# Values of two key tiles in a row, and x's rounding moved to ScalarE, in a fused Perceiver kernel

## The reference, cut to what matters

```
# quantised layer (_L0_ffn_ref), on layernorm(x)
scale = 127.0 / clip(max(abs(x), axis=-1), 1e-05)
x_q   = clip(round(x * scale), -128, 127) / scale
h     = (x_q @ w1_q.T) * s1 ; h = new_gelu(h)
out   = (quantised(h) @ w2_q.T) * s2

# large attention (_L1_xattn_ref): 16 heads, 64 queries, 1601 keys
q_r, k_r = rotated, projected queries and keys
attn  = softmax(einsum('bhsr,bhlr->bhsl', q_r, k_r))
ctx_c = einsum('bhsl,bld->bhsd', attn, kv_r)      # the "values"
out   = ctx_c through w_kc_kv and Wo
```

## Time and profile before

| what | us |
|---|---|
| median of 3 runs | 2840.44 |
| the profiled execution | 2837.08 |
| its span | 2835.2 |
| small attention and weights before the quantised layer | 0 to 331 |
| quantised layer | 331 to 466 |
| large attention | 466 to 2074 |
| second small attention | 2074 to 2200 |
| mixture of experts | 2200 to 2835 |

### The profile page before, as it was taken

One profiled execution on the slowest core, in us unless ns is written; L12 is line 12 of the kernel. 1 busy time (PEld: TensorE's weight loads), 2 busy tenths in 40 slices (PEclk: granted clock), 3 DMA queues, 4 the chain that ended last, 5 costly groups with the idle time before them and its releaser, 6 DMA issues. The chain is left out here.

```text
span 2835.2 us, 46672 instructions
## 1 busy us (share of the span) xinstructions
PE 2658.0 (94%) x16872; PEld 1648.4 (58%) x16872; DVE 1529.4 (54%) x2425; ACT 1110.6 (39%) x2096; POOL 1243.3 (44%) x668
## 2 busy tenths in 40 slices
PE   6989467999999999999999999999979899999999
PEld 4667345656655665666566566656446465656555
DVE  4757585565565556456555655655569633323322
ACT  4635363354445435444543544454435311111110
POOL 1033014577687778668766866776500000000000
PEclk9989698999999999999999999999999899999999
DMA  2000400110111101111110110110030111111111
GB/s 65 1 30 0 153 1 35 50 60 30 47 41 47 41 29 59 38 39 41 47 41 29 59 45 31 41 47 30 18 158 0 32 51 49 56 53 56 52 60 41
DMA packets 44051, 128.00 MB, mean 45 GB/s; under 512 B 6596, under 2 KB 11332, under 8 KB 42312
## 3 DMA queue, kind: packets, MB, share of 16 engines
q1 hardware_dynamic: 43032, 126.53, 13.8%
q10 hardware_dynamic: 944, 0.45, 0.1%
HBM read 85.20 MB, written 2.24 MB: 31 GB/s over the span
## 5 line engine op out<-in xcount | busy, mean ns | idle before, releaser
L716 POOL TENSOR_TENSOR cx_acc<-cx_acc,f_w 128x1024 f32<-128x1024 f32 x310 | 736.4, 2375 | 218.0 <-ACT f_w L1070 205.6
L1070 ACT ACTIVATE f_w<-cx_st 128x512 f32<-128x512 f32 x768 | 438.7, 596 | 447.2 <-PE cx_st L911 392.0
L1174 DVE TENSOR_REDUCE cx_mhalf<-cx_mx 128x1 f32<-128x804 f32 x512 | 480.9, 989 | 171.3 <-PE cx_mx L887 171.2
L922 PE MATMUL cx_av<-f_w,cx_kv 128*64 128x512 f32 x1536 | 412.1, 615 | 0.0
L910 PE MATMUL cx_st<-cx_q,cx_k 128*128 128x512 f32 (+1 forms) x832 | 367.4, 442 | 4.1 <-ACT cx_prob L1070 3.4
L911 PE MATMUL cx_st<-cx_q,cx_k 128*128 128x512 f32 (+1 forms) x832 | 328.9, 395 | 0.0
L887 PE MATMUL cx_mx<-cx_kp,cx_q 128*128 128x402 f32 x1024 | 297.2, 376 | 19.5 <-DVE cx_mhalf L1174 18.3
L887 PEld LDWEIGHTS cx_mx<-cx_kp,cx_q 128*128 128x128 f32 x1024 | 167.6, 189 | 200.2 <-DVE cx_mhalf L1174 183.4
L1996 DVE TENSOR_TENSOR moe_passed<-moe_silu,moe_up 128x512 f32<-128x512 f32 x112 | 76.9, 687 | 382.0 <-issue 356.1
L1917 ACT ACTIVATE moe_silu<-moe_gate 128x512 f32<-128x512 f32 x112 | 66.9, 597 | 490.8 <-PE moe_gate L1841 490.8
L910 PEld LDWEIGHTS cx_st<-cx_q,cx_k 128*128 128x128 f32 (+1 forms) x832 | 154.9, 186 | 170.4 <-ACT f_w L1070 136.4
(11 more groups left out here) (216 smaller groups left out, 3766.3 us busy)
## 6 DMA issues: line engine op xcount, KB each, us to landing
cx_k<-cx_kp SPq DMA_DIRECT2D x32, 804.0 KB, 3.9
moe_share<-moe_coef_kept SPq DMA_DIRECT2D x56, 256.0 KB, 3.0
cx_ctx<-in_cx_ctxN SPq DMA_DIRECT2D x32, 416.0 KB, 3.3
cx_ctxr<-in_cx_ctxrN SPq DMA_DIRECT2D x32, 416.0 KB, 3.9
cx_k<-cx_kp SPq DMA_DIRECT2D x32, 402.0 KB, 5.2
moe_wgu<-in_moe_wgu SPq DMA_DIRECT2D x7, 1024.0 KB, 11.0
moe_wd<-in_moe_wd SPq DMA_DIRECT2D x4, 896.0 KB, 22.3
moe_share<-moe_coef_kept SPq DMA_DIRECT2D x16, 224.0 KB, 2.9
```

The lines of the kernel that those rows point to most:

```text
L716: engine.tensor_tensor(acc[rows, :, :], sofar, prob[slot(kt)][rows, :, :], ALU.add).then_inc(s_acc, 1)
L922: last = pe.matmul(av[DCX * p:DCX * p + DCX, :], kv[e][0:nk(kt), kt, :], prob[slot(kt)][0:nk(kt), p, :], start=(kt == 0), stop=(kt == NKT ...
L1070: act.activation(prob[slot(kt)][rows, p, :], st[p][rows, :], ACT.Exp).then_inc(s_exp, 1)
L1174: dve.tensor_reduce(mhalf[:, i // 2, i % 2:i % 2 + 1], mx[i % 2][:, :, 0:KQ], AX.XY, ALU.max)\
```

## The change

In the large attention `VALUES_AT` lists, for even and odd batches, the steps in which `values` is issued. Where the step before is not in the list, its key tile is done first in the same place. Odd batches do the tiles (0,1), (2,3), (4,5), (6,7), (8,9), (10,11) in pairs at the end of steps 1, 3, 5, 7, 9 and 11, and tile 12 alone; even batches do (0,1), (2,3), (4,5) in pairs and 6 to 12 alone. `denominators` stays at the end of step 0.

In the quantised layer the multiplication and the first rounding of x go from VectorE (L1596) to a new `round_x` on ScalarE, with two new semaphores. VectorE's `quantise_x` is cut in two: `find_x_scale(t + 2)` now stands before `unscale(t + 1)`, and the rest of `quantise_x(t + 2)` at the end of the pass, behind `change_x` and `gather`.

```
+    VALUES_AT = ((1, 3, 5, 6, 7, 8, 9, 10, 11, 12), (1, 3, 5, 7, 9, 11, 12))
...
-                            values(n, e, kt)
+                            if kt in VALUES_AT[e]:
+                                if kt - 1 not in VALUES_AT[e] and kt > 0:
+                                    values(n, e, kt - 1)
+                                values(n, e, kt)
...
+            def round_x(t):                                    # ScalarE
+                act.wait_ge(s_xs, t + 1)
+                act.activation(xn[t % 2][:, :], xn[t % 2][:, :], ACT.Identity, bias=bias[:, 0:1],
+                               scale=inv[t % 2][:, 0:1]).then_inc(s_xr, 1)
...
+            round_x(0)
+            round_x(1)
             keep_y1T(0)
             keep_y1T(1)
             gelu(0)
...
                 for n in job_range(t, 0):
                     keep(n)
+                if t + 2 < NT:
+                    round_x(t + 2)
                 keep_y2T(t)
...
-            def quantise_x(t):                                 # VectorE
+            def find_x_scale(t):
...
-                step.done(scales(t, 0))
-                step.done(dve.tensor_scalar(xn[g][:, :], xn[g][:, :], inv[g][:, 0:1], ROUND, ALU.mult, ALU.add))
+                scales(t, 0).then_inc(s_xs, 1)
+
+            def quantise_x(t):
+                dve.wait_ge(s_xr, t + 1)
...
+            find_x_scale(0)
+            find_x_scale(1)
             quantise_x(0)
+            quantise_x(1)
             gather(2)
-            quantise_x(1)
             unscale(0)
             for t in range(NT):
                 find_scale(t)
+                if t + 2 < NT:
+                    find_x_scale(t + 2)
                 if t + 1 < NT:
                     unscale(t + 1)
                 quantise_hidden(t)
-                if t + 2 < NT:
-                    quantise_x(t + 2)
                 if t > 0:
                     change_x(t - 1)
                 if t + 3 < NT:
                     gather(t + 3)
+                if t + 2 < NT:
+                    quantise_x(t + 2)
```

More of the change, by code:

```diff
@@ L1420, in quantised_mlp @@
     s_rstd = sem("f0_rstd")
+    s_xs = sem("f0_x_scale_found")
+    s_xr = sem("f0_x_rounded")
     s_y1 = sem("f0_y1_quantised")
@@ L1586, in gather @@
                 dve.tensor_scalar(mv[t % 2][:, 1:2], mv[t % 2][:, 1:2], EPS, None, ALU.add).then_inc(s_var, 1)
-            def quantise_x(t):
+            def find_x_scale(t):
                 g = t % 2
                 dve.wait_ge(s_rstd, t + 1)
+                if t >= 2:
+                    dve.wait_ge(s_y1, t - 1)
                 step.done(dve.tensor_scalar(xn[g][:, :], x_all[:, t, :], mv[g][:, 0:1], rstd[g][:, 0:1],
@@ L1594, in quantise_x @@
                 step.done(dve.tensor_reduce(amax[g][:, 0:1], xn[g][:, :], AX.X, ALU.max, apply_absolute_value=True))
-                step.done(scales(t, 0))
-                step.done(dve.tensor_scalar(xn[g][:, :], xn[g][:, :], inv[g][:, 0:1], ROUND, ALU.mult, ALU.add))
+                scales(t, 0).then_inc(s_xs, 1)
+            def quantise_x(t):
+                dve.wait_ge(s_xr, t + 1)
                 if t >= 2:
                     dve.wait_ge(s_y1T, t - 1)
-                dve.tensor_scalar(y1[g][:, :], xn[g][:, :], ROUND, 127.0, ALU.subtract, ALU.min).then_inc(s_y1, 1)
+                dve.tensor_scalar(y1[t % 2][:, :], xn[t % 2][:, :], ROUND, 127.0, ALU.subtract, ALU.min)\
+                    .then_inc(s_y1, 1)
             def unscale(t):
```

## The result

| what | before | after |
|---|---|---|
| median of 11 runs each on one chip, us | 2840.44 | 2852.65 |
| lowest to highest | 2835.08 to 2846.61 | 2846.25 to 2861.37 |
| ratio, with its 95% interval | | 1.0046 [1.0033, 1.006] |
| the profiled execution, us | 2837.08 | 2853.11 |
| large attention, first score matmul to the last matmul of the last `denominators` | 1550.8 | 1561.6 |

The forecast was +18, this is +12.

What follows compares the result with a forecast made beforehand. TensorE was taken to bound the large attention. Attention +17 and quantised layer +1 gave +18 on the profiled 2837.08, 2855; the runs' median lies 3.4 higher, so 2858 us, range 2840 to 2872.

Steps and rivals of the forecast that it cites:

- The saving per joint, 0.36: Large attention: joining two values groups saves 0.36 us of TensorE's switching between scores and values, if TensorE never waits.
- The gap of 1.57 in place of 1.03: Steps without values: the next score waits for the exp until 1.57 to 1.74 us; TensorE is ready at 1.03.
- (0,1) gains nothing: Odd batches: joining values 0 and 1 leaves the number of switches the same, as `denominators` then stands alone.
- third rival: Odd steps 0, 1, 2, 4: ScalarE's query copies or the two-wait way back also delay; +42, 2882 us; chance 0.07.
- (6,7), (8,9), even (4,5): the reduces: Joints in steps with pieces: VectorE's reduces hold up TensorE; +0.29, about +0.2 and +0.25 us.
- (10,11), -0.2: Odd batches, no pieces: turned keys of 0.4 us in the gap nearly cover the wait, so -0.2 us.
- The last batch, +1.5: Large attention's last batch: no pieces and no turned keys, so five joints at 0.29 each, +1.5 us.
- The sum of the attention, +17: Large attention: fifteen batch pairs at +1.07 give +16, last batch +1.5, batch 0 -0.4; +17 us, bounds -18 to +32.
- The quantised layer, +1: Quantised layer: `down` waits for the hidden row's copy behind the new rounding; -1 to +2 us, taken as +1.
- the ring I named: Quantised layer's pass, 7.00 us: unscale, `y2`, x's quantisation, `change_x`, `down`, turned `y1`, its copy, `up`, next unscale.
- No change: Rival: the wait of 0.65 us is covered about half; -5 to +5 us, 2835 to 2846; chance 0.09.
- the plain drain saving: Rival: drain saved and the wait doesn't show, -41 us, 2799; or -18, 2822, with exps late; chance 0.10.

Runs made afterwards that it cites:

- e3: Kernel before with only tiles (10,11) of odd and (7,8) of even batches joined, quantised layer as before: 2823.61 us, ratio 0.9934.
- e4: Changed attention, layer as before, plus two unread matmuls of 402 columns at the end of odd steps 2 and 4: 2852.95 us.
- e11: Kernel before with only tiles (0,1) and (2,3) of odd batches joined: 2839.58 us against a single 2847.63.
- e12: Kernel before with only tiles (2,3) of odd batches joined: 2854.27 us.
- e6: Changed attention, layer as before, each piece reduced over 402 of its 804 elements: 2787.44 us.
- e8: Kernel before with only tiles (10,11) of odd batches joined: 2831.65 us against 2838.21 before on that chip.
- e1: Kernel before with all the change's joined values, quantised layer as before: 2852.72 us against 2841.29, ratio 1.0037.
- e2: Kernel before with the change's quantised layer part alone, values one by one: 2839.86 us, ratio 0.9994.
- e5: Kernel before plus two unread matmuls of 402 columns at the end of odd steps 2 and 4: 2853.75 us.

## Why the prediction was right, and where its sizes were off

- **The saving per joint, 0.36.** Right: 0.33 where it shows nearly undisturbed (e3).
- **The gap of 1.57 in place of 1.03.** Right to the last digit in these steps, by the trace and by e4. The slower way back, 1.74, does not occur in these steps.
- **(0,1) gains nothing.** Right as a sum. That it shields (2,3) was not seen; e11 and e12 show it, worth 0.38. The reason given against the third rival ("a copy starts behind the second exp and has the 1.87 of the pair ... to hide in") holds only because of it. That part was luck: without the pair (0,1) each odd batch would have lost 0.38 more, about 6 us in all.
- **(6,7), (8,9), even (4,5): the reduces.** Right: 0.25, 0.19 and 0.26 against 0.29, 0.2 and 0.25; e6 turns all three into gains.
- **(10,11), -0.2.** This term was mis-sized: -0.14 for the joint and -0.44 for the stall at the border behind it, which the prediction did not price at all. Together that is 0.38 more than was forecast, 0.38 x 15 = 5.7 us, the largest part of the miss. e8 shows it alone.
- **The last batch, +1.5.** The distance between its `denominators` does grow by 1.48 (25.38 to 26.86), but 0.91 of that is the first values group, which used to stand ahead of the first of them and now stands behind. The rest is 0.57: five joints at 0.15 to 0.18, less 0.27 at tile 12. They cost less than 0.29 because the gap there is 1.42 and not 1.57:

```profile
2067.85 1.94 PE L923 MATMUL cx_av<-f_w,cx_kv 128*64 128x512 f32 x8
2069.72 0.50 PE L911 MATMUL cx_st<-cx_q,cx_k 128*128 128x512 f32 x1
2070.06 0.39 PE L912 MATMUL cx_st<-cx_q,cx_k 128*128 128x512 f32 x1
...
2071.14 0.50 PE L911 MATMUL cx_st<-cx_q,cx_k 128*128 128x512 f32 x1 [0.22 <-ACT f_w L1074]
```

```profile
2070.49 1.09 ACT L1074 ACTIVATE f_w<-cx_st 128x512 f32<-128x512 f32 x2 [1.92 <-PE cx_st L912]
```

  The exp starts 0.04 behind the end of the scores (2070.06 + 0.39), not 0.19 as in the earlier trace rows and in the odd steps above. The trace shows what stands between. In batches 1 to 28 ScalarE works out, in a register, the number that each of the exp's further two waits (L1072, L1073) compares with, and it does so after the wait for the scores; in batches 0 and 29 to 31 it does not. Line L1072 has 13 such instructions in each of the 28 batches, 364 in all; 350 of them are this row (number, nanoseconds, first and last start), the other 14 a second form of 37 ns:

```profile
L1072 ACTq ALU_OP  x350: 35/35/35, 578.3 to 1966.9; - x175
```

  At the joint (2,3) shown above, the scores end at 1081.37, the two register instructions start at 1081.41 and 1081.48, and the exp at 1081.56. So 0.15 of each exposed gap of 1.57 is the loop's own bookkeeping. A kernel without it was not run.
- **The sum of the attention, +17.** Measured +10.8: 14 x 0.76, the last pair +0.53 (78.96 to 79.49; its odd batch is 29, with the shorter gap), the last batch +0.57, and batch 0 -1.0 (first score to first `denominators` 62.36 to 60.48, less the same 0.91). The -1.0 of batch 0 is not the -0.4 that was forecast, and it is not the change. It arises between the first score and the end of the values of tile 1, 8.22 us before and 7.19 after, where the granted clock was 0.61 and 0.71. e8 and e12, whose batch 0 is as before, take 7.05 and 7.03 there at 0.73, and e11, also as before, takes 8.23 at 0.61. From there to the end of the values of batch 0 it is 52.11 before and 52.17 after. Without this accident of the clock the attention would be longer by about 12, as the medians and e1 say.
- **The quantised layer, +1.** The mechanism was right: `down` waits for the copy and the copy for the rounding. A pass at the full clock even became 0.10 shorter, and e2 finds no difference. Whether the sum is +1 or -1 can't be told. The mark that I set, "if the quantised layer moves by over 3 us, the ring I named is not the bound", was a bad one: without any change in it the layer takes from 132.6 (e3, clock 0.82) to 140.8 us (e5, clock 0.75).
- **The signs.** The score rows have their bracket, 0.37 where about half a us was named; the wait for the reduces in (6,7) and the 1.87 of a pair are there; two batches grow by 0.76, not 1.1. One sign did not come: ScalarE's exps at these places are still in pairs ("x2"), since both scores end before the second exp is due.
- **The rivals.** No change and the plain drain saving (the rule that a mode switch drains the array, taken alone) are excluded by the interval of the ratio, which begins at 1.0033, and so is rival 3's +42, though its mechanism is real. The Trainium skill (TensorEngine Tiling (Array Packing), "Key Properties") tells of the drain. In e3 joints with work in the gap give it back, nearly in full at (7,8), 0.33 of 0.36, and in part at (10,11), 0.12; the other half of e3's gain is the border's stall.

## What to carry to other kernels

Before putting groups of the same array arrangement together, ask what the group that is moved away was covering: here 1.01 us of values hid most of a round trip over another engine of 1.57, and the joint paid only where other matmul work stood in that gap, or where the longer lump hid an old stall. Price each place by itself, since joints of one kind were worth from -0.58 to +0.33 each in one kernel, and read every row that shows a wait twice: once for its latency and once as something that could be won. Taking only two joints that pay turned +12 into -18 us.

## What the runs showed of the hardware that was not expected

- TensorE's granted clock in the quantised layer differs from profile to profile where nothing in the layer was changed: 0.82, 0.78, 0.76 and 0.74, with 132.6, 136.8, 138.3 and 139.5 us. Single executions can't be compared over this stage to better than some 8 us (the longest, e5, took 140.8).
- Two matmuls of 402 columns in the gap between two dependent score groups cost nothing (99.63 against 99.59), and 0.37 us where TensorE was never waiting.
- An exp that waits for scores starts 0.19 us behind them in batches 1 to 28 and 0.04 in batches 0 and 29 to 31. The 0.15 is two register instructions of 0.035 each, starting 0.07 apart, that work out what the exp's other waits compare with.
- A reduce of 804 elements (988 ns) in place of one of 402 (574 ns in e6) costs the kernel before 2.20 us per two batches and the changed one 3.66, though VectorE is idle for almost half of the time.
